# An attention and mixture-of-experts block on one core: token lists and 39 tiles of listed rows in place of eight dense experts

## What is computed

```
x = x + _layernorm(attn(_layernorm(x)))
x = x + _layernorm(ffn(_layernorm(x)))
...
logits = jnp.einsum('td,ed->te', xf.astype(jnp.float32), gate_w)
probs = jax.nn.softmax(logits.astype(jnp.float32), axis=-1)
weights, indices = jax.lax.top_k(probs, K)
weights = (weights / weights.sum(-1, keepdims=True)).astype(x.dtype)
combine = jnp.einsum('tk,tke->te', weights, onehot)
g = jnp.einsum('td,edh->teh', xf, w_gate)
u = jnp.einsum('td,edh->teh', xf, w_up)
h = jax.nn.silu(g) * u
out = jnp.einsum('teh,ehd,te->td', h, w_down, combine)
sgate = jax.nn.sigmoid(xf @ shgate_w)[:, None]
sh = jax.nn.silu(xf @ shw_gate) * (xf @ shw_up) @ shw_down
out = out + (sgate * sh)
```

## Time and profile before

| | us |
|---|---|
| median of 3 runs (802.46 to 802.77) | 802.72 |
| the profiled execution | 803.5 |
| its span in the trace | 801.7 |
| PE, PEld, DVE busy | 740.5, 699.0, 706.7 |
| ACT, POOL busy | 539.8, 447.8 |

### The profile page before, as it was taken

The page is one execution under the profiler, slowest core; times in us unless marked ns, Lnnn a source line. Parts: engine busy times, 40 slices in busy tenths (PEclk is TensorE's granted clock), DMA queues, the critical chain, the costliest instruction groups (busy, mean ns, idle before and its releaser), DMA issues.

```text
span 801.7 us, 16636 instructions
## 1 busy us (share of the span) xinstructions
PE 740.5 (92%) x5184; PEld 699.0 (87%) x5184; DVE 706.7 (88%) x2359; ACT 539.8 (67%) x2142; POOL 447.8 (56%) x456
## 2 busy tenths in 40 slices
PE   2559999999999999999999998689999999999996
PEld 2448999999999999998998997579999999999996
DVE  7799999999999999999999989888877788777875
ACT  5859999999999998998998998513233223333231
POOL 4977888788887888878878887351100101001000
PEclk9889999999999999999999999879999999999999
DMA  7006000000000000000000002100000000000000
GB/s 300 0 27 233 2 2 1 2 1 2 2 1 2 2 1 1 2 1 2 2 1 2 1 1 80 40 0 8 8 7 8 8 15 7 8 8 9 14 8 14
DMA packets 5846, 16.70 MB, mean 21 GB/s; under 512 B 640, under 2 KB 2816, under 8 KB 5504
## 3 DMA queue, kind: packets, MB, share of 16 engines
q1 hardware_dynamic: 5760, 15.64, 5.4%
HBM read 13.54 MB, written 2.10 MB: 20 GB/s over the span
## 4 chain that ended last, share of the span: by engine, by line
PE 61%; DVE 28%; ACT 9%; issue 1%; DMA 1%; SPq 0%; POOLq 0%; POOL 0%; DVEq 0%; ACTq 0%
PE pQ L279 6%; PE pQ L280 6%; PE pQ L281 6%; PE pS L279 4%; PE pS L281 4%; PE pS L280 4%; PE pO L279 4%; PE pO L281 3%; PE pO L280 3%; PE pT L419 3%; DVE PT L802 3%; PE pP L347 3%; PE pA L279 2%; DVE osb L828 2%; DVE aT L807 2%; DVE qT L781 2%
## 5 line engine op out<-in xcount | busy, mean ns | idle before, releaser
L1050 POOL TENSOR_SCALAR lr<-mv 128x1 f32<-128x1 f32 (+1 forms) x48 | 9.3, 193 | 243.2 <-DVE mv L822 148.1
L279 PE MATMUL pQ<-WQ,hT 128*128 128x512 f32 (+4 forms) x388 | 135.1, 348 | 9.8 <-DVE t L771 6.6
L280 PE MATMUL pQ<-WQ,hT 128*128 128x512 f32 (+4 forms) x388 | 132.6, 342 | 0.0
L281 PE MATMUL pQ<-WQ,hT 128*128 128x512 f32 (+4 forms) x388 | 132.1, 340 | 0.0
L1069 POOL TENSOR_TENSOR t<-t 128x640 f32<-128x640 f32 x64 | 100.5, 1570 | 56.0 <-DVE t L771 56.0
L614 ACT ACTIVATE vh<-pT 128x384 fp32r<-128x384 f32 (+1 forms) x80 | 37.4, 468 | 139.8 <-PE pT L419 139.8
L539 ACT ACTIVATE P<-P,nmx 128x128 f32<-128x128 f32 (+1 forms) x256 | 118.6, 490 | 0.7 <-DVE nmx L792 0.6
L547 ACT ACTIVATE P<-P,rinv 128x128 f32<-128x128 f32 (+1 forms) x256 | 105.2, 476 | 15.0 <-DVE rinv L798 15.0
L1077 POOL TENSOR_TENSOR t<-t,tables 128x640 f32<-128x640 f32 x64 | 102.2, 1597 | 5.0
L279 PEld LDWEIGHTS pQ<-WQ,hT 128*128 128x128 f32 x388 | 76.3, 197 | 14.9 <-DVE t L771 7.6
L524 ACT ACTIVATE t<-pQ 128x128 f32<-128x128 f32 x320 | 87.9, 298 | 0.0
(11 more groups left out here) (149 smaller groups left out, 2677.1 us busy)
## 6 DMA issues: line engine op xcount, KB each, us to landing
stage<-in_wqkv SPq DMA_DIRECT2D x3, 768.0 KB, 8.4
X<-in_x SPq DMA_DIRECT2D x8, 256.0 KB, 4.7
out<-X SPq DMA_DIRECT2D x16, 128.0 KB, 1.7
stage<-in_wd SPq DMA_DIRECT2D x1, 1792.0 KB, 11.7
X<-in_wo SPq DMA_DIRECT2D x1, 1536.0 KB, 13.1
stage<-in_gu SPq DMA_DIRECT2D x2, 768.0 KB, 5.9
tables<-in_gu SPq DMA_DIRECT2D x2, 768.0 KB, 5.0
stage<-in_wqkv SPq DMA_DIRECT2D x2, 384.0 KB, 3.9
```

Source lines behind the costliest of these rows:

```text
L279: e.matmul(out, lh, rh, start=start, stop=False, skip_group_check=True)
L280: e.matmul(out, lh, rl, start=False, stop=False, skip_group_check=True)
L281: return e.matmul(out, ll, rh, start=False, stop=stop, skip_group_check=True)
```

## The change

The shared expert stays dense. The eight experts no longer see every token: each token's normalized row is written to the lists of its two experts in a DRAM tensor `xs`, 39 tiles of 128 listed rows are read back, each goes through one expert, and the results are written to a DRAM tensor `ys` at 2 x token + choice. At the end the two rows of a token and the shared part are added. `SEQ` now has three kinds of slots:

```diff
-SEQ = [(0, LC), (1, LC)]
-for _m in range(NT):
-    SEQ += [(_m, 0), (_m, 1)] + ([(_m + 1, LC)] if 1 <= _m < NT - 1 else []) + [(_m, 2), (_m, 3)]
+NRT = (TOPK * NTOK - NE) // 128 + NE
+RING = 8
+XRING = 8
+YRING = 4
+SLOT0 = 135
+SEQ = [("G", m) for m in range(7)] + [("U", 0), ("G", 7), ("U", 1), ("G", 8), ("U", 2), ("G", 9), ("G", 10), ("U", 3)]
+SEQ += [("G", m) for m in range(11, 16)] + [("U", m) for m in range(4, 8)]
+SEQ += [("R", j) for j in range(NRT)] + [("U", m) for m in range(8, 16)]
+CHUNKS = [(0, 4), (4, 8), (8, 12), (12, 14), (14, 16)]
+ROUTE_AT = {AT["G", b - 1] + 1: c for c, (a, b) in enumerate(CHUNKS)}
+PLACE_AT = {AT["G", b - 1] + 2: c for c, (a, b) in enumerate(CHUNKS)}
+SCATTER_AT = {AT["G", b - 1] + 3: c for c, (a, b) in enumerate(CHUNKS)}
+PAIR_AT = {AT["U", 8] + 2 + p: p for p in range(NPAIR)}
```

Routing works on chunks of two or four tiles (`route`, `places` on DVE). Then POOL writes rows by indirect DMA; rows live in a ring of eight tiles, whose second copy SP makes by a DMA inside SBUF:

```diff
+            def ln2_apply(m):
+                b, t = divmod(m, 2)
+                e.wait_ge(s_nb2, b + 1)
+                if m >= RING:
+                    c = CHUNK_OF[m - RING]
+                    e.wait_ge(s_scat[c], 32 * (CHUNKS[c][1] - CHUNKS[c][0]))
...
+            def scatter(c):
+                a, b = CHUNKS[c]
+                e.wait_ge(s_slots, c + 1)
+                e.wait_ge(s_wsig, 2 * c + 2)
+                e.wait_ge(s_tail, c + 1)
+                e.wait_ge(s_zeroed, 96)
+                for m in range(a, b):
+                    e.wait_ge(s_h2row, m + 1)
+                    wait_copied(e, m)
+                    for k in range(2):
+                        e.indirect_dma_start(xs_d[:, :], bass.IndirectOffsetOnAxis(ap=slots[:, k, m:m + 1], axis=0),
+                                             rows[:, m % RING, k, :], None).then_inc(s_scat[c], 16)
```

After the last chunk `tile_list` (DVE) makes the table of the 39 tiles; SP waits for it and for all scatters, reads each tile's row from the table into a register (`value_load`) and loads it. PE reads the place of the expert's weights in the same way:

```diff
+            def load_xg(j):
+                if j >= XRING:
+                    e.wait_ge(*ys_done(j - XRING))
+                    e.wait_ge(s_xT, j - XRING + 1)
+                if j >= 4:
+                    e.wait_ge(s_dxg[j % 4], 16 * (j // 4))
+                r = e.value_load(rlist[0:1, 0, j:j + 1], min_val=0, max_val=NROW - 128)
+                e.dma_start(xg[j % XRING], xs_d[bass.ds(r, 128), :]).then_inc(s_dxg[j % 4], 16)
...
+            def x_T(j):
+                e.wait_ge(s_dxg[j % 4], 16 * (j // 4 + 1))
...
+                place_of[j] = e.value_load(rlist[0:1, 1, j:j + 1], min_val=EAT, max_val=EAT + (NE - 1) * EW)
```

`r_up` is 6 matmuls of 352 columns, `r_down` 5 of 256. `r_twice` (POOL) copies 48 columns of the activation, so that its last rows stand twice in the second stationary tile. `r_out` on ACT scales by the token's weight, on POOL it scatters to `ys`. The end of the program:

```diff
+            for j in range(NRT - YRING, NRT):
+                e.wait_ge(*ys_done(j))
+            def load_yl(p):
+                for m in (2 * p, 2 * p + 1):
+                    e.dma_start(yl[m], ys_d[2 * 128 * m:2 * 128 * (m + 1), :].rearrange(
+                        "(p k) c -> p (k c)", k=2)).then_inc(s_dyl[max(p - 3, 0)], 16)
+
+            for p in range(RING // 2):
+                load_yl(p)
+            for p in range(NPAIR):
+                e.wait_ge(s_fres, p + 1)
+                if p + RING // 2 < NPAIR:
+                    load_yl(p + RING // 2)
+                e.dma_start(out_d[:, 2 * p:2 * p + 2, :], X[:, 2 * p:2 * p + 2, :]).then_inc(s_out, 16)
```

More of the change, by code:

```diff
@@ L162, in program @@
[L162 to L174, removed]
+        sw_raw = part(stage, 0, SWN)
+        ew_raw = [part(stage, z * EH, EH) for z in range(3)]
+        sgb = [part(stage, 3648 + i * NSH, NSH) for i in range(2)]
+        actb = [part(stage, 4352 + i * NSH, NSH) for i in range(2)]
+        rc = part(stage, 5056, 296)
+        zrow = part(stage, 5352, RW)
@@ new lines, in last_add, with ffn @@
+            def last_add(p):
+                e.wait_ge(s_fapp, p + 1)
+                for t in range(2):
+                    m = 2 * p + t
+                    a = e.tensor_tensor(X[:, m, :], X[:, m, :], yl[m][:, 0:HID], ALU.add)
+                a.then_inc(s_fres, 1)
+            def ffn(q):
+                kind, i = item(q + 5)
+                if kind == "G" and i % 2 == 0:
+                    ln2_stats(i // 2)
+                kind, i = item(q + 2)
+                if kind == "G":
+                    ln2_lo(i)
+                kind, i = item(q + 1)
+                if kind == "R":
+                    x_lo(i)
+                kind, i = item(q)
+                if kind == "G":
+                    gate(i)
+                elif kind == "U":
+                    up(i)
+                elif kind == "R":
+                    r_silu(i)
+                kind, i = item(q - 1)
+                if kind == "U":
+                    up_lo(i)
+                elif kind == "R":
+                    r_lo(i)
+                kind, i = item(q)
+                if kind == "R":
+                    r_act(i)
+                if q in ELO_AT:
+                    ew_half(ELO_AT[q])
+                if q in ROUTE_AT:
+                    route(ROUTE_AT[q])
+                if q in PLACE_AT:
+                    places(PLACE_AT[q])
+                    if PLACE_AT[q] == LASTC:
+                        tile_list()
+                if q in PAIR_AT:
+                    last_sum(PAIR_AT[q])
+                if q - 3 in PAIR_AT:
+                    last_add(PAIR_AT[q - 3])
@@ L1045, in _ @@
+                if s == ZERO:
+                    router_constants()
+                ffn(s - SLOT0)
+                if s == STEPS - 1:
+                    out_stats(NB - 1)
+            out_scale(NB - 1)
+            out_add(NB - 1)
+            for q in range(STEPS - SLOT0, SEND):
+                ffn(q)
         @block.gpsimd
```

1189 lines of the change are left out of this document (740 added, 449 removed).

## The result

| | before | after |
|---|---|---|
| median (4 runs each) | 802.73 us | 821.66 us (818.01 to 822.35) |
| ratio to before, 95% interval | 1 | 1.0227 (1.0197 to 1.0258) |
| span of the profiled execution | 801.7 us | 819.4 us |

What follows compares the result with a forecast made beforehand. It took the dense experts as bound by TensorE alone. First routed product at 603 us, 103 us of routed tiles and 66.5 us for the end gave a 772.5 us span, about 774 us predicted against 803.5; range 726 to 840 us.

Steps and rivals of the forecast that it cites:

- the first part: From step 135 at 507 us to the first routed tile's up product, forecast at 603 us.
- a): Slots 0 to 5 and the rest of attention, up to the first scatter: 19 us on DVE, to 526 us.
- c): Slots 7 to 10, between ACT's two waits for scatters: 16 us on DVE, with a second routing step.
- f): Last 16 scatters, 16T + 2, then register and xs load (3), first transpose, copy and low half (1).
- T: Time for POOL to issue one indirect DMA of 128 rows, taken as 1.2 us.
- b) and d): ACT's two waits until eight scatters have landed and free the row buffers: 8T + 2 each.
- rival 1: POOL's issue of indirect DMAs becomes the bound; slower, 853 us at T = 3; chance 0.13.
- The second part: The 39 routed tiles, bound by PE at 2.65 us each: 103 us, to 706 us.
- rival 2: Routed tiles run at 1.2 GHz, a slot costing 2 us more; slower, 852 us; chance 0.11.
- rival 3: Issue and register load nearly free, T = 0.4 and 2.1 us a routed tile; 726 us; chance 0.13.
- The third part: The end after the last routed up product: 66.5 us, with four turns of 7.9 us, to 772.5 us.
- rival 4: Spare indices not through by 526 us, so the lists start late; say 810 us; chance 0.03.

Runs made afterwards that it cites:

- e1: The changed kernel with stage columns for raw expert weights laid out so that experts 0 and 1 load early: 811.19 us.
- e6: The changed kernel with PE doing the feed-forward slot first in a step, ahead of its attention work: 809.89 us.
- e11: e8_all with the first feed-forward slot one step later, in step 136: 750.63 us.
- e9: e8_all with the weights of experts 6 and 7 split in slots 11 and 13 in place of 8 and 9: 758.81 us.
- e8_all: The changed kernel with the edits of e1, e2, e5 and e6, eight chunks of two tiles, and one semaphore per pair's loads at the end: 759.66 us.
- e3: The changed kernel with only 16 of the 32 row scatters issued, leaving out every token's second expert: 800.34 us (one run).
- e4: The changed kernel with routed tile j's expert fixed as j mod 8, so PE loads no register: 814.24 us (one run).
- e5: The changed kernel with 128 rows in place of 64 in the last down matmul of a routed slot: 818.15 us.
- e10: e8_all with ten buffers for loaded list tiles in place of eight: 752.89 us.
- e2: The changed kernel with last_add called before last_sum in each slot of the end: 809.16 us.

## Why the prediction was wrong

**The step that failed** is the first part, "from step 135 (507 us, taken as unmoved ...) to the first R", by 47 us: it summed the busy time of one engine where every engine waited for the one before it. In its own terms:

- *"taken as unmoved; ... I allow 5 us either way"*: 10.3 us. I had listed where the weights are split but not asked what each split's load waits for. The load waits on POOL, ACT on the load (8.5 us), the softmax on ACT. e1 gives 10.5 us back.
- *a), 19 us by the sum of DVE's work*: it took 39.4. DVE was busy 17.56 of 40 us from 520 to 560, so its work was not sized too low, and it was not the bound. In a step PE's transposes and gate product come behind pv, ACT's sigmoid behind that, the next `probs_hi` behind the sigmoid, DVE's `probs_lo` and the next pv behind that: a ring of handoffs, with three table loads of 1.28 us in it and PE at clock 0.79. I had put the table loads "at nothing ... in steps in which ACT is a third busy"; an idle engine is no cover when the others wait for it: of the table load of 528.16 us, 0.8 us lie inside PE's wait of 2.42 us. e6 (11.8 us) shows the ring, 12.4 us of the 20.7. What the table loads and PE's clock cost in all is open: e11 (9.0 us) has fewer table loads and less of the ring at once, and no run changes the clock alone.
- *c), 16 us*: 23.1. 3.8 us of `out_scale` held by POOL fall in it; e9 found such a hold to be worth nothing measurable, though on e8_all, where the chunks are smaller, so for after it is not shown. This part was not taken apart further.
- *f), 16T + 2, load 3, first transpose, copy and low half 1*: 7.2 us more. 1.0 is T at 1.26 in place of 1.20, another 1.5 the gaps between the last three blocks of scatters. The largest piece is that behind the first list tile's transposes PE has three parts of shared tiles in its queue, at 1.2 GHz (starts 0.29 us apart for 352 columns, where full speed has 0.16): 4.8 us from 645.15 to 649.91 before the first routed up product. I had followed the tile, not the queue of the engine it arrives at.
- *b) and d), 8T + 2 each*: 11.9 and 11.5 us for a forecast of 11.6. T is 0.96 us in the instruction and 0.30 between two: 1.26 us, against 1.2. This, the term that I held to be the risk (rival 1), was right, and e3 shows that the scatters count in full. That it was right is in part luck: 1.2 was taken from an unlike operation, between bounds of 0.33 and 3.5.

**The second part** was right in the sum (99.6 us for 103) by luck, two errors that cancel: the register load costs 0.15 us, not 0.6 (e4), and a slot without it takes 2.40, not 2.02. The trace puts 0.29 us of PE's time in a slot into the step to 64 rows and back (e5), of which only 0.10 came out of the period until e10 opened the ring of loads. From 650 to 750 us the clock is 1.00: rival 2 did not happen, nor did rival 3.

**The third part** was right: 69.9 us for 66.5, turns of 7.7 for 7.9, and 10.2 us of wait for the first loads. The prediction described this ring and e2 opens it.

**Costed at nothing**: the zero fill landed in 62.5 us, where the estimate had 113, and the spare indices were issued by 165 us, so they delayed nothing: the attention masks near 480 us stand some 1.5 us earlier than before, and rival 4 did not happen. The last sentence of that paragraph, on table loads, is the one that was wrong. *The rule against the change* added nothing that shows in the scatters: their issue took 0.96 to 1.23 us.

**Among the rivals** the slow ones named POOL's issue and the clock of the routed tiles. What happened was neither, and no rival had it: handoffs that nothing covered, ahead of the routed tiles. The observed time lies inside the range, which the slow rivals had widened, but on the side that I gave 0.25, and not for their reasons.

**Slips in the working**, none of which decides: by the slope 352 columns take 0.160 us, not 0.158; the pieces of a routing step add up to 3.7 us at most, not 3.8; the forecast case, with all its terms at their ends, spans 740 to 818 us, not 745 to 802, and the kernel after lies above that too.

## What to carry to other kernels

Where a bound stage is replaced by one in which no engine is full, a sum of busy times per engine is only a floor: follow one item through the in-order queues, with everything that stands ahead of it at each, table loads and matmuls at half clock included. Ask of every load what frees its buffer, and of every call in a loop over slots whether the one behind it could go first. Better placed and more buffers, two swaps of calls, a semaphore for each pair's loads, finer chunks, 128 rows in one matmul and one more step of delay turned 2.3% slower into 7.4% faster, and their gains added up.

## What the runs showed of the hardware

An indirect DMA of 128 rows of 258 words keeps POOL 0.96 us (the first of a block 1.0 to 1.2) and the next starts 0.30 us behind its end; it lands 2.5 us after its issue. Scatters of 256 words to `ys` keep POOL 0.98 us. A matmul on 64 rows between matmuls on 128 costs 0.29 us more than one on 128 (e5), so doing less work took longer. Two DVE scalings that take 0.73 us together take 4.51 beside two of POOL's subtractions (e9). A register load on PE takes 0.30 us in the queue; without it and its register instructions the period is 0.15 us shorter (e4). The fill of `xs`, 17,415 KB from one row of 1032 bytes on each partition of SBUF, took 62.5 us, some 285 GB/s.
